# Four cross-attention layers: the wide layers' values multiplied with the output weights before the probabilities are

## The chip, the cores and the metric

The kernel runs on one core of one Trainium2 chip. The metric is the device time of one execution in microseconds. Three runs of the kernel before took 2065.84 to 2066.42 us, with a median of 2066.3 us.

## What is computed

The stream `x` has 8 batches of 512 tokens with 512 channels, the context 8 batches of 77 rows with 1024 channels. Four layers follow each other. Layers 0 and 2 are the wide ones (16 heads of 64, a token bias, an output bias), 1 and 3 the narrow ones (16 heads of 32, four groups of keys and values, a root-mean-square norm on the queries' side).

```
def wide(x, ctx):                      # L0, L2
    q, k, v = heads64(x @ Wq), heads64(ctx @ Wk), heads64(ctx @ Wv)
    probs = softmax(q @ k.T * 64 ** -0.5 + col_bias)
    return merge(probs @ v) @ Wo + bo + x
def narrow(x, ctx):                    # L1, L3
    q, k, v = heads32(rmsnorm(x) @ wq), groups4(ctx @ wk), groups4(ctx @ wv)
    return merge(softmax(q @ k.T * 32 ** -0.5) @ v) @ wo + x
```

All is float32 in the reference. The kernel splits each operand into a high part in fp32r and a rest, and multiplies in three passes: high by high, high by rest, rest by high.

## The kernel before

**Context phase.** `context_part` runs nine rounds `j`: eight form the keys and values of four heads of a wide layer (`k_scr`, `v_scr` in DRAM), the ninth those of both narrow layers. In a round TensorE makes four key chains (banks 0 to 3, 8 channel chunks of 3 passes of 308 columns each: 96 multiplications) and five value chains (banks 4 to 7, 8 chunks of 3 passes of 256 columns: 120 multiplications). ScalarE copies a bank's high part out (`drain_keys`, `drain_values`) and VectorE forms the rest; both also split the next round's weights, which SyncE loads. In round 0 VectorE forms the token bias (a chain of 39 small instructions on lines 498 to 516) before it drains the first keys. Only the start of round 1 waits for these key drains.

**Main phase.** 128 units `u`, 32 to a layer: a batch has four units of four heads. Step `s` of the program holds the scores of unit `s` (four tiles of 128 tokens by 4 x 77 columns), the queries of unit `s+1`, the transposes of unit `s-1`, and probabilities times values of unit `s-2`. Each engine has its order written out by hand. For a unit TensorE makes

- scores: 24 multiplications of 154 columns (wide) or 12 of 308 (narrow),
- queries: 24 or 12 of 512 columns,
- transposes (`turn`): three blocks of four, 128 columns each; the third block holds the columns that don't fit into the first two,
- probabilities times values (`values`): 8 of 512 columns in either kind,
- the output projection (`project`): 96 in a wide batch, 48 in a narrow one, of 512 columns.

VectorE subtracts the maxima (`tile_scores`), forms the denominators, and the rests of queries, transposes and head outputs (`rest_q`, `rest_t`, `rest_o`), and adds the result to the stream (`add_result`). ScalarE makes the exponentials and the high parts. GpSimd normalises the probabilities (`normalise`), gathers the third block of wide units (`rest`) and forms the rests of the stream and of weights. A transpose waits for the bank's readers two transposes before; a score tile waits for VectorE's subtraction two tiles before, and in wide layers also for ScalarE's bias (`s_biased`). The exponentials of a narrow layer wait for `rstd`, which GpSimd makes after TensorE's `stats`. In narrow steps the addition of a projection is left to the next step (`late`).

## Time and profile before

| | |
|---|---|
| median of three runs | 2066.3 us |
| the profiled execution, its own time | 2066.7 us |
| its span, first to last instruction | 2064.9 us |
| mean granted clock of TensorE | 0.996 |
| context phase | 0 to 262 us |
| layers 0, 1, 2, 3 begin (first scores) | 268, 782, 1148, 1681 us |
| TensorE busy | 2024.2 us, 98% |
| VectorE, ScalarE, GpSimd busy | 68%, 47%, 31% |

Matmuls are pipelined, and the busy time of one is longer than its distance to the next; the distances between starts are what adds up. PE is TensorE's multiplications, PEld its weight loads, DVE VectorE, ACT ScalarE, POOL GpSimd, SPq the DMA issues of SyncE.

### The profile page before, as it was taken

To read this page: it belongs to the slowest core of one execution; us is meant where nothing else is said; L and a number is where in the kernel's file an instruction comes from. 1 tells how busy PE (TensorE), PEld (TensorE's weight loads), DVE (VectorE), ACT (ScalarE), POOL (GpSimd) and SP (SyncE) were. 2 spreads that over 40 slices of the span, in tenths; PEclk is the share of its full clock that TensorE was granted. 3 is DMA by queue.
4 is the path that set the end of the run, shared out by engine and by line. 5 is a ranking of instruction groups with operands and counts; after the bars stand their busy time and mean duration, and the time that the engine had idled before them with its cause. 6 is when DMAs were issued, how large, how long until landed. Compare 5 with 4: busy or idle time off the path is not lost.

```text
span 2064.9 us, 31181 instructions
## 1 busy us (share of the span) xinstructions
PE 2024.2 (98%) x11482; PEld 1760.5 (85%) x11482; DVE 1398.2 (68%) x2408; ACT 966.0 (47%) x1814; POOL 649.5 (31%) x534
## 2 busy tenths in 40 slices
PE   8999999999999998999999999999999989999998
PEld 8999988888888887788888888888888877888887
DVE  5332365775577557788888676557755775888886
ACT  3222354544355354555555454345443553555553
POOL 1000043311232244454444431223122543444441
PEclk9999999999999999999999999999999999999999
DMA  7889742222122222343333332222221222333332
GB/s 196 183 176 200 191 97 67 68 65 79 51 72 71 70 71 74 89 107 100 87 98 94 101 96 68 72 60 67 66 79 52 72 77 81 74 92 92 88 72 84
DMA packets 262537, 191.02 MB, mean 93 GB/s; under 512 B 197522, under 2 KB 199986, under 8 KB 259826
## 3 DMA queue, kind: packets, MB, share of 16 engines
q1 hardware_dynamic: 262386, 189.03, 35.7%
q8 instruction: 92, 1.51, 0.3%
q14 instruction: 59, 0.48, 0.1%
HBM read 132.66 MB, written 56.26 MB: 91 GB/s over the span
## 4 chain that ended last, share of the span: by engine, by line
PE 48%; issue 30%; POOL 11%; DVE 6%; ACT 2%; DMA 1%; SPq 1%; POOLq 0%; DVEq 0%; ACTq 0%
PE acc_bank L877 6%; POOL prob L1311 6%; PE acc_bank L261 4%; PE t_bank L857 4%; PE acc_bank L263 4%; PE acc_bank L262 4%; PE q_bank L835 4%; PE q_bank L837 3%; PE q_bank L839 3%; PE ctx_bank L261 3%; PE ctx_bank L262 3%; PE ctx_bank L263 3%; POOL x_s L1286 3%; PE s_bank L261 2%; POOL rest L1320 2%
## 5 line engine op out<-in xcount | busy, mean ns | idle before, releaser
L1311 POOL TENSOR_TENSOR prob<-prob,rinv 128x1232 f32<-128x1232 f32 x128 | 288.3, 2252 | 1006.3 <-DVE rinv L1195 1006.2
L1053 ACT ACTIVATE q_s<-q_bank 128x512 fp32r<-128x512 f32 x192 | 114.7, 597 | 489.3 <-PE q_bank L839 486.2
L877 PE MATMUL acc_bank<-pT_s,vals_s 128*128 128x512 f32 x1024 | 337.8, 415 | 0.0
L835 PE MATMUL q_bank<-x_s,w_s 128*128 128x512 f32 x768 | 319.4, 416 | 0.0
L1153 DVE TENSOR_REDUCE mx<-s_bank 128x4 f32<-128x308 f32 x512 | 240.1, 469 | 108.6 <-PE s_bank L801 54.3
L837 PE MATMUL q_bank<-x_s,w_s 128*128 128x512 f32 x768 | 313.3, 408 | 0.0
L839 PE MATMUL q_bank<-x_s,w_s 128*128 128x512 f32 x768 | 313.1, 408 | 0.0
L261 PE MATMUL acc_bank<-o_s,w_s 128*128 128x512 f32 x752 | 300.4, 400 | 2.8 <-DVE o_s L1186 2.5
L263 PE MATMUL acc_bank<-o_s,w_s 128*128 128x512 f32 x752 | 293.6, 390 | 0.0
L262 PE MATMUL acc_bank<-o_s,w_s 128*128 128x512 f32 x752 | 293.1, 390 | 0.0
L1044 ACT ACTIVATE prob<-prob,rstd 128x308 f32<-128x308 f32 x256 | 140.7, 553 | 263.2 <-DVE prob L1157 238.0
L1157 DVE TENSOR_TENSOR prob<-s_bank,mx 128x308 f32<-128x308 f32 x512 | 245.0, 478 | 27.4 <-DVE mx L1153 1.4
L1180 DVE TENSOR_TENSOR pT_s<-t_bank,pT_s 128x512 fp32r<-128x512 f32 x256 | 175.6, 686 | 78.5 <-ACT pT_s L1067 78.5
L877 PEld LDWEIGHTS acc_bank<-pT_s,vals_s 128*128 128x128 f32 x1024 | 191.0, 189 | 28.1
L1209 DVE SCALAR_TENSOR_TENSOR x_back<-acc_bank,bo,x_back 128x512 f32<-128x512 f32 x64 | 47.8, 748 | 244.9 <-PE acc_bank L263 244.9
L1067 ACT ACTIVATE pT_s<-t_bank 128x512 fp32r<-128x512 f32 (+1 forms) x320 | 183.1, 589 | 34.3 <-PE t_bank L857 34.2
L857 PE MATMUL t_bank<-ident,prob 128*128 128x128 f32 (+1 forms) x1280 | 184.7, 273 | 1.2 <-DVE pT_s L1180 1.2
L1192 DVE TENSOR_REDUCE sums<-prob 128x16 f32<-128x1232 f32 x128 | 182.5, 1426 | 0.0
L857 PEld LDWEIGHTS t_bank<-ident,prob 128*128 128x128 f32 (+1 forms) x1280 | 154.6, 135 | 28.0 <-DVE pT_s L1180 1.6
L261 PEld LDWEIGHTS acc_bank<-o_s,w_s 128*128 128x128 f32 x752 | 141.4, 188 | 31.2 <-DVE o_s L1186 4.4
L263 PEld LDWEIGHTS acc_bank<-o_s,w_s 128*128 128x128 f32 x752 | 141.2, 188 | 30.6
L839 PEld LDWEIGHTS q_bank<-x_s,w_s 128*128 128x128 f32 x768 | 145.5, 189 | 23.0
(107 smaller groups left out, 4092.8 us busy)
## 6 DMA issues: line engine op xcount, KB each, us to landing
stream<-x_back SPq DMA_DIRECT2D x128, 256.0 KB, 2.6
x_front<-stream SPq DMA_DIRECT2D x96, 256.0 KB, 3.3
x_back<-stream SPq DMA_DIRECT2D x96, 256.0 KB, 4.0
kvw_raw<-kvw SPq DMA_DIRECT2D x17, 1024.0 KB, 8.4
k_scr<-k_out SPq DMA_DIRECT2D x36, 308.0 KB, 10.5
keys_s<-k_scr SPq DMA_DIRECT2D x128, 77.0 KB, 2.5
v_scr<-v_out SPq DMA_DIRECT2D x8, 1024.0 KB
vals_s<-v_scr SPq DMA_DIRECT2D x512, 6.5 KB
```

The lines of the kernel that those rows point to most:

```text
L261: pe.matmul(out, weights[0], moving[0], start=start, stop=False)
L262: pe.matmul(out, weights[0], moving[1], start=False, stop=False)
L263: return pe.matmul(out, weights[1], moving[0], start=False, stop=stop)
L835: pe.matmul(out, w[0], x_now[0], start=k == 0, stop=False)
L837: pe.matmul(out, w[0], x_now[1], start=False, stop=False)
L839: mm = pe.matmul(out, w[1], x_now[0], start=False, stop=k == XC - 1)
L857: mm = pe.transpose(t_bank[(3 * u + n) % 2][0:rows, t * P:t * P + P], p, ident[:, :])
L877: mm = pe.matmul(out, w, pT_s[:, part], start=i == mine[0] and part == 2 * n and w is v[0], stop=i == mine[-1] and w is terms[-1][0] and p ...
L1067: act.activation(pT_s[0:rows, 2 * n], t_bank[(3 * u + n) % 2][0:rows, :], ACT.Copy).then_inc(t_hi, 1)
L1153: dve.tensor_reduce(top, scored, AX_X, ALU.max).then_inc(s_max, 1)
L1157: dve.tensor_tensor(prob[:, slot, t].rearrange("q (h n) -> q h n", h=GH), scored, top.unsqueeze(2).broadcast_to([P, GH, CTX]), ALU.subtrac ...
L1311: pool.tensor_tensor(view, view, rinv[:, slot].unsqueeze(2).broadcast_to([P, TILES * GH, CTX]), ALU.mult).then_inc(p_norm, 1)
```

## The change

In the wide layers (probs @ v) @ Wo becomes probs @ (v @ Wo), head by head. The product v @ Wo has 4 x 77 rows of 512 columns for each batch and group of four heads. It is formed for all batches in the context phase and kept in DRAM.

- **Context, rounds 0 to 7.** The five value chains go. Four chains like the keys' give the values turned, in the key chains' banks 0 to 3: chain n waits until the drain of key chain n of the same round is done (`k_lo`), and the next round's key chain n for the turned values' drain (`vt_lo`). The high part of a head lies in 64 partitions and its rest in the other 64, with Wo in both, so that two multiplications give all four products.
- **Context, rounds 1 to 8.** Between the chain steps TensorE makes 20 outputs of the round before (5 row blocks, 4 heads), two multiplications of 512 columns each, in banks 4 to 7. ScalarE drains the even ones, VectorE the odd ones into a ring of three 1 MB blocks, from which SyncE stores them. That is 616 x 4 rows of 2048 bytes for a round, 5.05 MB. Wo is loaded and split once for a round. The keys are stored with 2464 bytes in a row (308 before). Round 8 keeps five value chains for the narrow layers, in banks 0 to 3. The ring lies where the first query weights go afterwards, so that their split waits for its last stores.
- **Wide layers.** `project` and `values` go. Two units are taken together: their 616 probability rows make five blocks (four of 128, one of 104), and for each of four output chunks TensorE makes 15 multiplications of 512 columns, 60 for two units. Half of a pair's chunks stand in each of steps u+3 and u+4. SyncE loads 256 columns of the product for both units, ScalarE and GpSimd split two chunks of 640 columns for a step (`split_rows`, `rest_rows`), VectorE adds the bank to the stream (`add_wide`). `rest_o` and `split_o` go there. The value products now stand beside the scores of tiles 0 and 1, the queries beside those of tiles 2 and 3. Steps 0 to 2 and 64 to 66 have none.
- **Transposes, all layers.** The third block of two units is transposed together, after the second: 20 transposes for two units (24 before). GpSimd gathers it for narrow units too. In a narrow pair VectorE takes two pieces of 64 partitions out of the shared bank; the even unit's last two value products wait for it, and its drain moves to the next step.
- **Narrow additions.** `late` holds for odd steps only; in even steps VectorE adds the projection at the step's end.
- **Weights.** Wo of the wide layers is no longer streamed in the main phase.

```diff
 
-WEIGHTS = [("woA0", 0, 2, (0, 0, 1, 1)), ("woA1", 0, 3, (2, 2, 3, 3)),
-           ("wqB", 0, 0, (29, 29, 29, 29)), ("woB", 0, 1, (32, 33, 34, 35)),
-           ("wqA0", 1, 2, (36, 37, 38, 39)), ("wqA1", 1, 3, (40, 41, 42, 43)),
-           ("woA0", 1, 0, (63, 64, 65, 65)), ("woA1", 1, 1, (67, 67, 68, 68)),
-           ("wqB", 1, 2, (93, 93, 93, 93)), ("woB", 1, 3, (96, 97, 98, 99))]
+WEIGHTS = [("wqB", 0, 2, (12, 13, 14, 15)), ("woB", 0, 3, (16, 17, 18, 19)),
+           ("wqA0", 1, 0, (37, 38, 39, 40)), ("wqA1", 1, 1, (41, 42, 43, 44)),
...
+    def wide(self, s):
+
+        u = (s - 3) // 2 * 2
+        if not 0 <= u < NU or kind(u).name == "B":
+            return []
+        return [(u, 2 * (s - 3 - u) + i) for i in range(2)]
...
+    def split_values(self, u):
+
+        return self.narrow(u) and u % 2 == 0
+
+    def turns(self, u):
+
+        if not 0 <= u < NU:
+            return ()
+        if u % 2 == 0:
+            return 0, 1
+        return (0, 1, TWICE) if kind(u).name == "A" else (0, TWICE, 1)
...
+    def outs_after(j, step):
+
+        if j == 0:
+            return []
+        return [i for i in range(OUTS) if (8 + 5 * i // 2 if j < LAST else 6 + 3 * i // 2) == step]
+
...
+        def store_rows(j, r):
+            block = NV * j + r
+            sp.wait_ge(vw_act, 2 * block + 2)
+            sp.wait_ge(vw_dve, 2 * block + 2)
+            for b, t0, t1, row in ROW_PIECES[r]:
+                sp.dma_start(vw_scr[j, b, :, t0:t1].rearrange("h t c -> t h c"),
+                             staged[row:row + t1 - t0, block % 3].rearrange("p (h c) -> p h c", h=GH))\
+                  .then_inc(vw_stored[block % 3], 16)
+
...
+
+            act.wait_ge(wo_loaded, 32 * (j + 1))
+            if j:
+                act.wait_ge(vw_mm, OUTS * j)
+            act.activation(wd[:, 0], wo_raw[:, :], ACT.Copy).then_inc(wo_hi, 1)
 
         def drain_keys(n, j):
...
+        def drain_turned(n, j):
+
+            m, into, cols = n // 2, vt[j % 2], slice(n % 2 * HALF, (n % 2 + 1) * HALF)
+            act.wait_ge(vt_mm, 4 * j + n + 1)
+            if n == 0 and j >= 2:
+                act.wait_ge(vw_mm, OUTS * (j - 1))
+            act.activation(into[0:64, 2 * m, cols], banks[n][0:64, 0:HALF], ACT.Copy)
+            act.activation(into[64:P, 2 * m + 1, cols], banks[n][64:P, 0:HALF], ACT.Copy).then_inc(vt_hi, 1)
+
+        def drain_outputs(j, outs):
+
+            for i in outs:
+                if i % 2 == 0:
+                    block, h = NV * (j - 1) + i // GH, i % GH
+                    act.wait_ge(vw_mm, OUTS * (j - 1) + i + 1)
+                    if h == 0 and block >= 3:
+                        act.wait_ge(vw_stored[block % 3], rows_stored(block - 3))
+                    rows = VROWS[i // GH]
+                    act.activation(staged[0:rows, block % 3, 512 * h:512 * h + 512], banks[4 + i % 4][0:rows, :], ACT.Copy)\
+                       .then_inc(vw_act, 1)
...
+                act.wait_ge(vw_mm, OUTS * (LAST - 1))
+            elif n == 1:
+                act.wait_ge(wo_lo, LAST)
+                for block in range(NV * LAST - 3, NV * LAST):
+                    act.wait_ge(vw_stored[block % 3], rows_stored(block))
             act.activation(late_parts(n)[0], w_raw[:, n % 2], ACT.Copy).then_inc(late_hi, 1)
...
+        def chain_step(slot, n, k):
+
...
+        def outputs(j, step):
+
+            for i in outs_after(j, step):
+                r, h = divmod(i, GH)
+                if i == 0:
+                    pe.wait_ge(vt_lo, 4 * j)
+                    pe.wait_ge(wo_lo, j)
+                before = OUTS * (j - 1) + i - 4
+                if before >= 0:
+                    pe.wait_ge(vw_dve if i % 2 else vw_act, before // 2 + 1)
+                out = banks[4 + i % 4][0:VROWS[r], :]
+                v = vt[(j - 1) % 2][:, h, r * P:r * P + VROWS[r]]
+                pe.matmul(out, v, wd[:, 0, 512 * h:512 * h + 512], start=True, stop=False)
+                pe.matmul(out, v, wd[:, 1, 512 * h:512 * h + 512], start=False, stop=True).then_inc(vw_mm, 1)
...
+                chain_step(0, n, k)
         for j in range(NJ):
+            step = 0
             if j:
                 pe.wait_ge(w_lo[0], j)
-                pe.wait_ge(k_lo, 4 * j)
                 for n in range(4):
+                    pe.wait_ge(vt_lo, 4 * (j - 1) + n + 1)
                     for k in range(KC):
-                        keys(n, k)
+                        chain_step(0, n, k)
+                        outputs(j, step)
+                        step += 1
+            else:
+                step = 4 * KC
             pe.wait_ge(w_lo[1], j + 1)
-            for r in range(NV):
-                values(r, j)
+            if j < LAST:
+                for n in range(4):
+                    pe.wait_ge(k_lo, 4 * j + n + 1)
+                    for k in range(KC):
+                        chain_step(1, n, k)
+                        outputs(j, step)
+                        step += 1
+            else:
+                for r in range(NV):
+                    if r < 4:
+                        pe.wait_ge(k_lo, 4 * j + r + 1)
+                    else:
...
+                    sp.wait_ge(acc_mm, plan.acc[("pv", u - 2, 0)] + 1)
                 vals = vals_s[:, slot].bitcast(F32)
-                for h, t0, t1, blk, row, (first, last) in kind(u).pieces:
...
+            def load_rows(s):
+
+                if not plan.wide(s):
+                    return
+                u, m = plan.wide(s)[0]
+                half, b, p = plan.chunk(u, m) // 2, u // GROUPS % B, u // (2 * UNITS)
+                if half >= 2:
+                    sp.wait_ge(rows_lo, 2 * half - 2)
+                if u % UNITS == 0:
+                    sp.wait_ge(rows_zeroed, u // (2 * UNITS) + 1)
+                into, cols = rows_s[:, half % 2], slice(P * m, P * (m + 2))
+                for e in range(2):
+                    src = vw_scr[4 * p + (u + e) % GROUPS, b].rearrange("h t c -> (h t) c")
+                    sp.dma_start(into[:, 2 * e:2 * e + 2], src[0:2 * P, cols].rearrange("(n q) c -> q n c", q=P))\
+                      .then_inc(rows_loaded[half % 2], 16)
+                    sp.dma_start(into[REST * e:REST * (e + 1), 4], src[2 * P:SC, cols])\
+                      .then_inc(rows_loaded[half % 2], 16)
 
...
-                    pe.wait_ge(p_gathered, plan.gathered(u))
+                    if u == 0:
+                        pe.wait_ge(context.v_lo, len(VROWS))
+                item = plan.t[(u, n)]
+                after(pe, t_lo, item - 1)
+                if n == TWICE:
+                    pe.wait_ge(p_gathered, u + 1)
...
+            def wide_values(s):
+
+                for u, m in plan.wide(s):
+                    n, item = plan.chunk(u, m), plan.acc[("pv", u, m)]
...
-                            mm = pe.matmul(out, w, pT_s[:, part], start=i == mine[0] and part == 2 * n and w is v[0],
-                                           stop=i == mine[-1] and w is terms[-1][0] and part == terms[-1][1])
-                            if i == mine[-1] and w is terms[-1][0] and part == terms[-1][1]:
-                                mm.then_inc(acc_mm, 1)
...
+                        if m == 0:
+                            pe.wait_ge(t_lo, wide_turn(u, block) + 1)
+                        rows, p = BROWS[block], wide_block(u, block)
+                        w = [ring(n)[0:rows, h, block] for h in range(2)]
+                        pe.matmul(out, w[0], p[0:rows, 0], start=block == 0, stop=False)
+                        yield
+                        pe.matmul(out, w[0], p[0:rows, 1], start=False, stop=False)
+                        yield
+                        mm = pe.matmul(out, w[1], p[0:rows, 0], start=False, stop=block == BLOCKS - 1)
+                        if block == BLOCKS - 1:
...
                     for t in range(TILES):
                         beside(scores(s, t), q, 6)
-                        if t >= 2:
-                            turned(t - 2)
-                    turned(2)
+                        if t == 2:
+                            turned(turns[:2])
+                    turned(turns[2:])
                 elif a:
                     half = 12 if kind(s + 1).name == "A" else 6
-                    beside(scores(s, 0), q, half)
-                    beside(scores(s, 1), q, half)
-                    beside(scores(s, 2), v, 4)
-                    turned(0)
-                    beside(scores(s, 3), v, 4)
-                    turned(1)
-                    turned(2)
-                    for gb, m in plan.projections(s):
-                        project(gb, m)
+                    run(wide, 6)
+                    run(v, 6 if behind else 8)
+                    beside(scores(s, 0), wide, 12)
+                    beside(scores(s, 1), wide, 12)
+                    beside(scores(s, 2), q, half)
+                    if not behind:
+                        projected(projections)
+                    turned(turns[:2])
+                    beside(scores(s, 3), q, half)
+                    turned(turns[2:])
                     if plan.stats_at(s) is not None:
                         stats(plan.stats_at(s))
+                    if behind:
+                        projected(projections[:1])
+                        run(v, 2)
...
-                    turned(1)
+                    run(v, 3 if behind else 5)
+                    turned(turns[1:2])
                     if plan.stats_at(s) is not None:
                         stats(plan.stats_at(s))
-                    turned(2)
-                    if not plan.ahead(s):
-                        for gb, m in plan.projections(s):
-                            project(gb, m)
+                    turned(turns[2:])
+                    if behind:
+                        projected(projections[:1])
+                        run(v, 2)
+                        projected(projections[1:])
+                    else:
+                        projected(projections)
                 elif s == NU:
-                    run(v, 9)
-                    for gb, m in plan.projections(s):
-                        project(gb, m)
-                    turned(0)
...
+            def split_rows(n):
+
+                act.wait_ge(rows_loaded[n // 2 % 2], 64 * (n // 4 + 1))
+                if n >= CHUNKS:
+                    act.wait_ge(acc_mm, plan.chunk_item(n - CHUNKS) + 1)
+                if n // (2 * UNITS) and n % (2 * UNITS) < CHUNKS:
+                    act.wait_ge(acc_mm, plan.acc[("proj", 2 * B - 2, XC - 1)] + 1)
+                act.activation(ring(n)[:, 0], raw_rows(n), ACT.Copy).then_inc(rows_hi, 1)
 
...
+            def add_wide(u, m):
+
+                item, gb, p = plan.acc[("pv", u, m)], u // GROUPS, u // (2 * UNITS)
                 out, here = acc_bank[item % 2][:, :], x_back[:, m]
-                if kind(GROUPS * gb).name == "A":
+                dve.wait_ge(acc_mm, item + 1)
+                if u % GROUPS == 0:
+                    dve.wait_ge(back_loaded[m], 16 * (gb + 1))
                     dve.scalar_tensor_tensor(out=here, in0=out, scalar=bo[:, p, m:m + 1], in1=here,
                                              op0=ALU.add, op1=ALU.add).then_inc(acc_out, 1)
                 else:
+                    dve.wait_ge(acc_out, plan.acc[("pv", u - 2, m)] + 1)
                     dve.tensor_tensor(here, out, here, ALU.add).then_inc(acc_out, 1)
 
...
+                        rest_o(s - 2)
+                    tile_scores(s, 2)
+                    if kind(s + 1).name == "A":
                         next(q, None)
-                    tile_scores(s, 1)
+                    if not behind:
+                        added(projections)
+                    turned(turns[:2])
+                    tile_scores(s, 3)
                     next(q, None)
-                    tile_scores(s, 2)
-                    if pv == 2:
-                        rest_o(s - 2, 0)
-                    turned(0)
-                    tile_scores(s, 3)
-                    turned(1)
-                    if pv:
-                        rest_o(s - 2, pv - 1)
...
-                    if s >= 1 and not plan.rest_later(s - 1):
-                        rest_t(s - 1, TWICE)
...
+                        add_wide(u, m)
+                    turned(turns[:1])
+                    if s < NU and not wide:
                         denominators(s)
                     next(q, None)
                     next(q, None)
...
+                    turned(turns[2:])
+                    added(projections)
             for m in range(XC):
                 dve.wait_ge(end_mm, m + 1)
...
+                if u >= 2:
+                    pool.wait_ge(t_mm, plan.rest_read_before(u))
+                size = REST if kind(u).name == "A" else REST_B
+                pool.tensor_copy(rest[:, :, size * slot:size * slot + size], prob[:, slot, :, SC - size:SC])\
+                    .then_inc(p_gathered, 1)
+
+            def rest_rows(n):
+
+                pool.wait_ge(rows_hi, n + 1)
+                pool.tensor_tensor(ring(n)[:, 1], raw_rows(n), ring(n)[:, 0].bitcast(F32), ALU.subtract).then_inc(rows_lo, 1)
 
```

## Rows read from the trace of the kernel before

**Rows 1.** The page's first part: busy time, share of the span, instructions of each engine.

```profile
PE 2024.2 (98%) x11482; PEld 1760.5 (85%) x11482; DVE 1398.2 (68%) x2408; ACT 966.0 (47%) x1814; POOL 649.5 (31%) x534
```

**Rows 2.** Busy time by stretch: stretch, length, each engine (instructions), granted clock, DMA share, GB/s.

```profile
80.00:160.00 80.00, 80.00 (x626) 80.00 (x626) 24.85 (x32) 21.28 (x32) 0.00 (x0) 1.00 0.85 175
867.00:1076.00 209.00, 208.66 (x1123) 178.12 (x1122) 178.56 (x322) 119.34 (x223) 103.55 (x72) 1.00 0.37 98
...
407.00:474.35 67.35, 67.35 (x369) 57.85 (x368) 44.84 (x77) 30.64 (x60) 17.00 (x17) 1.00 0.25 68
```

**Rows 3.** Timeline of TensorE, context phase: start, us, engine, line, tiles, count.

```profile
23.45 0.28 PE L261 MATMUL ctx_bank<-w_s,ctx_s 128*128 128x256 f32 x1
...
66.92 0.30 PE L261 MATMUL ctx_bank<-ctx_s,w_s 128*128 128x308 f32 x1
...
80.53 0.28 PE L261 MATMUL ctx_bank<-w_s,ctx_s 128*128 128x256 f32 x1
...
94.71 0.31 PE L261 MATMUL ctx_bank<-ctx_s,w_s 128*128 128x308 f32 x1
```

**Rows 4.** Timeline of TensorE, main phase: 24 query multiplications, eight transposes, what follows.

```profile
262.16 0.40 PE L835 MATMUL q_bank<-x_s,w_s 128*128 128x512 f32 x1
...
267.64 0.23 PE L795 MATMUL s_bank<-keys_s,q_s 128*128 128x154 f32 x1
...
1158.52 1.04 PE L857 MATMUL t_bank<-ident,prob 128*128 128x128 f32 x8
1159.31 0.48 PE L261 MATMUL acc_bank<-o_s,w_s 128*128 128x512 f32 x1
```

**Rows 5.** Timeline of ScalarE, then of VectorE, in the first context round.

```profile
22.39 1.70 ACT L415 ACTIVATE k_out<-ctx_bank 128x308 fp32r<-128x308 f32 x4 [4.61 <-PE ctx_bank L263]
23.98 1.91 ACT L408 ACTIVATE w_s<-kvw_raw 128x2048 fp32r<-128x2048 f32 x1
...
31.66 0.30 DVE L516 SCALAR_TENSOR_TENSOR bias_s<-ctx_raw,mask_b,bias_s 128x77 f32<-128x77 f32 x1
32.00 1.64 DVE L464 TENSOR_TENSOR k_out<-ctx_bank,k_out 128x308 fp32r<-128x308 f32 x4
33.55 2.28 DVE L458 TENSOR_TENSOR w_s<-kvw_raw,w_s 128x2048 fp32r<-128x2048 f32 x1
```

**Rows 6.** Groups by shape, 0 to 400 us: count | busy, mean ns | idle before.

```profile
L261 PE MATMUL ctx_bank<-ctx_s,w_s 128*128 128x308 f32 x288 | 89.0, 309 | 7.5 <-DVE ctx_s L484 7.5
...
L261 PE MATMUL ctx_bank<-w_s,ctx_s 128*104 128x256 f32 x72 | 20.3, 282 | 1.4 <-DVE v_out L470 1.2
```

**Rows 7.** Busy time by stretch, around the first narrow unit of layer 1.

```profile
784.50:788.10 3.60, 0.10 (x2) 0.03 (x1) 3.39 (x8) 0.00 (x0) 2.98 (x3) 0.90 0.19 38
788.10:794.60 6.50, 6.50 (x20) 5.45 (x21) 4.29 (x8) 2.58 (x5) 1.23 (x2) 0.53 0.13 28
```

**Rows 8.** DMA busy tenths and GB/s in 40 slices of 0 to 280 us; issues: us to landing.

```profile
DMA  6954199995998199949992999299959953949931
GB/s 212 417 186 150 39 113 188 368 108 93 338 201 62 78 337 256 98 105 353 177 69 96 358 161 75 113 342 345 106 145 344 150 44 136 334 117 174 142 95 51
...
kvw_raw<-x_in SPq DMA_DIRECT2D x1, 1024.0 KB, 6.9
```

**Rows 9.** Timeline of VectorE, one narrow unit of layer 3 (idle before, and its releaser).

```profile
2011.43 0.48 DVE L1153 TENSOR_REDUCE mx<-s_bank 128x4 f32<-128x308 f32 x1 [0.49 <-PE s_bank L263]
...
2016.68 0.69 DVE L1180 TENSOR_TENSOR pT_s<-t_bank,pT_s 128x512 fp32r<-128x512 f32 x1 [0.51 <-ACT pT_s L1067]
2017.29 1.43 DVE L1192 TENSOR_REDUCE sums<-prob 128x16 f32<-128x1232 f32 x1
...
2020.77 0.69 DVE L1177 TENSOR_TENSOR pT_s<-t_bank,pT_s 64x512 fp32r<-64x512 f32 x1
...
2021.89 0.48 DVE L1153 TENSOR_REDUCE mx<-s_bank 128x4 f32<-128x308 f32 x1 [0.44 <-PE s_bank L263]
```

**Rows 10.** Timeline of TensorE: the second unit of layer 0 begins.

```profile
279.21 0.34 PE L795 MATMUL s_bank<-keys_s,q_s 128*128 128x154 f32 x1 [1.49 <-DVE q_s L1164]
```

791 lines of the change are left out of this document (447 added, 344 removed).

## The prediction

> **What bounds the kernel now.** I read the page's first part, then the busy time by stretch, then TensorE's timeline for the distances between starts, and last what TensorE waits for. TensorE is busy in 98% of the span [rows 1]. In the context phase it has no gap, nor in a steady wide batch (67.35 us), and in the narrow stretch 0.3 us of 209 [rows 2]. So the first thing to count is TensorE's instructions, at their distance from start to start; the second is who makes it wait in the 40.7 us of its idle time (2064.9 less 2024.2 [rows 1]), 7.5 of which are the first loads [rows 6].
>
> The distances: 96 key multiplications of 308 columns take 80.53 - 66.92 = 13.61 us, 0.142 each; 120 of 256 columns 94.71 - 80.53 = 14.18 us, 0.118 each [rows 3]. 24 of 512 columns take 267.64 - 262.16 = 5.48 us, 0.228 each; eight transposes and what follows them 0.79 us, so 0.109 for each distance between transposes and 0.03 from the last to another kind [rows 4].
>
> **TensorE's count, context.** Removed: 8 rounds x 120 x 0.118 = 113.3 us. Added: 8 x 96 x 0.142 = 109.1, and 8 rounds x 20 outputs x 2 x 0.228 = 73.0. Together +68.8 us. Nothing hides it: this stretch has no gap to fill [rows 2].
>
> **TensorE's count, main phase.** A wide unit loses 8 value and 24 projection products and gets 30, so 2 x 0.228 = 0.456 us less, over 64 units 29.2. All 128 units lose two transposes on average, 256 x 0.109 = 27.9 us. Together -57.1 us. The count alone therefore gives +68.8 - 57.1 = +11.7 us. The product saves little because its inner length is 308 per four heads where the head outputs' is 256; it pays off by what other engines lose, and those don't set the time now.
>
> In two sentences apart: the Trainium skill ("TensorE: Matmul & The Clock Gate", section "Back-to-back issue gap") gives columns / 2.4 + 2.5 ns, which is 216, 131, 109 and 56 ns for 512, 308, 256 and 128 columns where the trace has 228, 142, 118 and 109. By these the count would be +64.8 - 42.0 = +22.8 us; its section "LDWEIGHTS" (128 columns in 107 ns) agrees with the 109 of the transposes.
>
> **A new wait in round 0.** The turned values' chain n uses the bank of key chain n and waits for VectorE's drain of it. ScalarE has its part done at 24.0, but VectorE comes to its first key drain only at 32.00, behind the token bias [rows 5]. Before, the value chains had banks of their own and started at 23.45 [rows 3]. Now TensorE stands from 23.45 to 32.00 + 0.48 + about 0.1: 9.1 us. Queued behind are all its later work, and so everybody. After 3.6 us without work TensorE ran at half clock (1.2 GHz) for most of the next 6.5 us, granted 0.53 [rows 7]; that costs 6.5 x 0.47 = 3.1 us here too. The 1.4 us that the fifth value chain waited for a bank [rows 6] goes. Sum +10.8. Bounds: 0, if I misread the order, and +12.2, if the 1.4 stays.
>
> **Other waits in the context phase.** Each output has a wait on its bank's drain four outputs earlier, about 6 us; the longest that stands before it on either engine is a weight split, 1.91 + 2.28 [rows 5], so it is hidden in rounds 1 to 7. In round 8 the first stream tile is split ahead of the output drains. Its load is issued after the stores of round 7's last block and takes 6.9 us [rows 8]; TensorE has 3.4 us of steps left in the round (8 of 0.42) and then some 7 to its fifth output, while load and both halves of the split take 1.8 + 6.9 + 1.91 + 2.28 = 12.9. Drain and order on two engines make it +3.5, bounds 0 and +6. The stores: a round moves 5.05 MB of products, 2 of weights, 1 of Wo and 1.26 of keys, 9.3 MB in 36.5 us, 255 GB/s. Slices of this phase reached 338 to 417 [rows 8], so I take 0, and 3 us a round (+24) as the upper bound. SyncE waits for a block's drains with a weight load queued behind it; that load has 20 us of slack.
>
> **Wide layers, steady.** VectorE loses two head rests and a transpose rest per unit, ScalarE likewise; GpSimd gets about 3.3 us for two chunks, at 52 us busy in a wide batch's 67 before only 17.0 [rows 2]. The copies of a chunk are made a step ahead. A first product block waits for the third transpose's rest, which I place 1.3 us before it is needed. 0, bounds 0 and +9.
>
> **Narrow layers, steady.** A pair of units has 2 x 10.46 = 20.9 us (2021.89 - 2011.43 for one [rows 9]) and TensorE's share falls by 4 x 0.109 = 0.44. VectorE has 0.44 to 0.49 us to spare where a unit begins [rows 9]. In the even step it now takes two pieces of 64 partitions (0.69 each) instead of one, has the addition at the end instead of in the next step, and has lost one head rest: 0.7 us more in front of the next unit's maxima. That is 0.3 over its slack and meets a TensorE that is earlier by 0.1. I take 0.35 us of waiting in a pair, 28 pairs: +10. Bounds 0 and +20. So the narrow transposes' gain (half of 27.9) comes back for the most part.
>
> **Borders of the layers.** (a) Wide to narrow, twice: TensorE now waits 3.5 us at the first narrow unit and then runs at half clock [rows 7]. After the change the 1.4 us of rest copies and two more rests are gone from VectorE's tail, and 6.8 us of value products stand in each of the first three narrow steps. The wait falls to about 2, perhaps short enough to keep the clock: -7 each, -14. Bounds -20 and 0. (b) Narrow to wide, once: steps 64 to 66 have score tiles 0 and 1 with nothing beside them, and tile 2 waits for maxima, subtraction and bias of tile 0: 1.2 us in two of them, 3.5 in the one without narrow value products, less what is lost there now: +5, bounds +2 and +9. (c) Step 2 loses its value products. A unit there waited 1.49 us for its queries' rest [rows 10]: +1.6, bounds 0 and +3.
>
> **The sum**, against the profiled execution's 2066.7 us (span and 1.8 around it, 0.4 over the median): +11.7 + 10.8 + 3.5 + 0 + 10 - 14 + 5 + 1.6 = +28.6. It gives 2095.3, and as a median 2095 us, 1.4% slower.
>
> **The rivals.**
> - *The setup wait is hidden.* If VectorE reaches the key drains before TensorE needs them, 10.8 falls away: 2084. Against it stands VectorE's unbroken timeline up to 32.00 [rows 5]. Chance 0.12.
> - *The stores come late.* 5 MB a round in a ring of three blocks; where a store lands over 12 us after its drain, ScalarE and VectorE stop, and TensorE with them. At 2.5 us a round, +20: 2115. For it speaks that slices are full already [rows 8], against it that the key stores become eight times as long a run. Chance 0.12.
> - *VectorE sets the narrow layers.* It was busy 178.6 of 209 us [rows 2], and even steps get more. With 1.0 us of waiting for a pair instead of 0.35, +18 to +20: 2114. Chance 0.13.
> - *A transpose is not worth its distance.* If removing one gives back only the 0.03 us between kinds, the saving is 7 us instead of 27.9: 2116. The rows say otherwise, as transposes follow each other at 0.109 throughout. The Trainium skill's figure of the second part would put this rival at 2106. Chance 0.03.
> - *Faster: the other engines' relief empties the main phase of waits.* One mechanism, at the layers' borders: VectorE and ScalarE lose some 2 us in each wide unit, and if TensorE then nowhere waits, up to 40.7 - 7.5 - 1.4 = 31.8 us of idle time and 2 x 3.1 of half clock go. With the count (+11.7) and round 0 (+10.8) that gives 2051 at the utmost. It decides from 26.6 us of released waiting on (the 22.5 and the bound of 4.1); for that the borders' new holes and the narrow pairs must cost nothing. I set it at 2057. Chance 0.06, and 0.04 for stopping on the way, at 2066.
> - *The forecast:* 0.50.
>
> **Range and chances.** Two kernels can be told apart by about 0.2%, 4 us. The forecast's own low end takes the lower bounds of several terms, about 2074; its high end with the ring or the narrow layers at their bounds about 2122. The range 2074 to 2122 leaves out the faster case and the tails. Faster 0.06, within 0.2% 0.04, slower 0.90.
>
> **What would show it.** The first scores should move from 267.6 [rows 4] to 267.6 + 68.8 + 10.8 + 3.5 = 351 us. TensorE should have 2.7 us less in a steady wide batch, 64.6 instead of 67.35. A gap of 9 us must stand at 23.5 with VectorE's key rest as its releaser and half clock behind it. In narrow layers the gaps should come in every second unit, at tile 3, released by VectorE. If the stores were late, ScalarE's waits in rounds 1 to 8 would name the stores. The prediction is wrong if the context phase is not longer by 70 us or more, or if a wide batch doesn't get shorter.

## The result, and the profile after

The kernel after takes 2362.5 us (median of four runs, 2359.4 to 2368.1), the kernel before in the same job 2066.4. The ratio is 1.1435, with a 95% interval of 1.1411 to 1.1459. I had forecast 2095 us, 2074 to 2122. The direction was right; of 296 us more, 29 were foreseen.

The page of after, in its parts: busy time of the first part (answers [rows 1]); TensorE's busy tenths, its granted clock and the DMA share of the second part in 40 slices; three groups of the fifth.

```profile
PE 2122.7 (90%) x11226; PEld 1814.4 (77%) x11226; DVE 1387.9 (59%) x2360; ACT 1000.1 (42%) x1814; POOL 823.1 (35%) x643
...
PE   7979876799978899989898999988999998898988
...
PEclk9989987899989899999999999998999999999999
DMA  5766765322232233323323233322333333233222
...
L1082 PE MATMUL acc_bank<-pT_s,vals_s 128*128 128x512 f32 x512 | 152.4, 411 | 65.7 <-issue 56.4
...
L259 PE MATMUL ctx_bank<-ctx_s,w_s 128*128 128x308 f32 x544 | 170.7, 314 | 17.3 <-DVE k_out L552 10.3
...
L1319 ACT ACTIVATE o_s<-rows_s 128x640 fp32r<-128x640 f32 x128 | 93.2, 730 | 207.2 <-DMA rows_s<-vw_scr 204.6
```

TensorE is busy in 90% of a longer span: 243 us idle where it had 41. The holes are in three places of the tenths: the first eight slices (context phase), slices 12 to 14 (part of layer 0) and 27 and 28 (part of layer 2), and a little everywhere in the narrow layers. The span is 2366.1 us, 301.2 over before's 2064.9. By the first score of each layer, the parts are:

| | before | after | difference | forecast |
|---|---|---|---|---|
| first scores | 267.6 | 446.6 | +179.0 | +83.1 |
| wide layers 0, 2 | 514.5, 532.5 | 550.7, 563.4 | +67.2 | -36.6 |
| narrow layers 1, 3, with the end | 365.9, 384.4 | 394.3, 411.0 | +55.0 | -18.0 |

(Forecast, wide: -29.2, half of the transposes -14.0, +5, +1.6. Narrow: -14.0, +10, -14.) So all three parts went wrong, and each needs its own cause.

**Context phase.** First the stretch of 50 to 440 us by busy time (columns as in [rows 2]), then what waited in the first 450 us (engine, line, what for: us in total, times, longest), then two rows of TensorE's timeline: the gap of round 0, and the first scores.

```profile
50.00:440.00 390.00, 310.87 (x1876) 290.40 (x1875) 153.77 (x200) 130.03 (x200) 0.00 (x0) 0.89 0.63 199
```

```profile
ACT staged L488 <- DMA vw_scr<-staged: 139.9, 24, 18.4
...
PE ctx_bank L689 <- ACT staged L488: 67.3, 8, 14.1
PE s_bank L1162 <- DVE wq_s L583: 11.4, 1, 11.4
```

```profile
32.62 0.60 PE L259 MATMUL ctx_bank<-ctx_s,w_s 128*128 128x308 f32 x1 [10.30 <-DVE k_out L552]
...
446.59 0.23 PE L1003 MATMUL s_bank<-keys_s,q_s 128*128 128x154 f32 x1
```

TensorE, which had no gap in the 80 us of this phase that [rows 2] shows, is idle for 79 of 390 us. In 67.3 of them, eight waits of up to 14 us, it waits for ScalarE's drain of an output; ScalarE waits for the ring's stores. The other 11.4 us stand at the end of the phase: the split of the first query weights, which go where the ring was, waits 12.2 us on ScalarE for the ring's last stores. The DMA engines' mean share is 0.63 (the row's last number but one): by that number they are far from full, and the stores are late all the same. That contradiction is what the experiments had to settle. The gap of round 0 is there as forecast, 10.3 us for 9.1, behind VectorE's key rest; from 32.6 to 37.4 us the granted clock is 0.50.

**Layers 0 and 2.** A steady wide batch takes 559.08 - 493.95 = 65.13 us from start to start (67.35 before, 64.6 forecast), so the change does what it was to do there. But units 13 to 20 of layer 0, in which weights are split, take 18 to 25 us in place of 16. One of them, in the order of the cause: GpSimd's weight rest, SyncE's issues, ScalarE's copy of a product chunk, TensorE's next score tile.

```profile
671.32 1.32 POOL L1577 TENSOR_TENSOR w_s<-stage,w_s 128x512 fp32r<-128x512 f32 x1
```

```profile
672.66 0.34 SPq L929 DMA_DIRECT2D stage<-wqB  x1
...
673.99 0.46 SPq L918 DMA_DIRECT2D rows_s<-vw_scr  x1
```

```profile
680.04 0.74 ACT L1319 ACTIVATE o_s<-rows_s 128x640 fp32r<-128x640 f32 x1 [11.37 <-DMA rows_s<-vw_scr]
```

```profile
681.15 0.49 PE L1003 MATMUL s_bank<-keys_s,q_s 128*128 128x154 f32 x1 [5.80 <-ACT s_bank L1264]
```

SyncE issues the next weight piece when GpSimd's rest of the piece two before is done (672.64), and only behind it the loads of the product's rows. They land at 680.0. ScalarE has stood for them for 11.4 us, and the bias of a score tile, which TensorE needs, is queued behind that copy: 5.8 us.

**Narrow layers.** A pair of units takes 24.6 us (1100.60 to 1125.18; the steady ones 23.0 to 25.0) where before it took 20.9 to 21.7. The even unit begins at 1100.60, the odd one at 1115.01 (TensorE), and between them stand this gap of TensorE and this addition of VectorE:

```profile
1100.60 0.30 PE L259 MATMUL s_bank<-keys_s,q_s 128*128 128x308 f32 x1
...
1106.02 1.62 PE L1082 MATMUL acc_bank<-pT_s,vals_s 128*128 128x512 f32 x3 [2.08 <-issue]
...
1115.01 0.30 PE L259 MATMUL s_bank<-keys_s,q_s 128*128 128x308 f32 x1
```

```profile
1104.85 0.48 DVE L1410 TENSOR_TENSOR prob<-s_bank,mx 128x308 f32<-128x308 f32 x1
1105.24 0.68 DVE L1462 TENSOR_TENSOR x_back<-acc_bank,x_back 128x512 f32<-128x512 f32 x1
```

The profile names no releaser ("issue"), but the product starts 0.1 us after VectorE's addition of the step before ends (1105.92). In an even unit the last accumulator item ahead of the value products is the projection of the step before, whose addition is `late`: VectorE makes it behind all four score tiles. The gap is not at tile 3, where I had looked for it, but behind it.

### The profile page after: what moved, and what is told of

It reads as the page before. It is cut to its first block, busy times and chain, and to the rows that moved or that the text cites. A ratio compares the mean times of both kernels' runs of the same rounds, so it can differ in the third digit from the quotient of the medians.

```text
span 2366.1 us, 30805 instructions
## 1 busy us (share of the span) xinstructions
PE 2122.7 (90%) x11226; PEld 1814.4 (77%) x11226; DVE 1387.9 (59%) x2360; ACT 1000.1 (42%) x1814; POOL 823.1 (35%) x643
## 4 chain that ended last, share of the span: by engine, by line
PE 65%; DMA 11%; issue 8%; POOL 5%; SPq 5%; DVE 3%; ACT 2%; DVEq 0%; POOLq 0%; ACTq 0%
PE q_bank L1045 6%; PE q_bank L1047 6%; PE q_bank L1049 6%; DMA vw_scr<-staged 6%; PE acc_bank L1082 5%; PE t_bank L1066 5%; PE acc_bank L1099 5%; PE acc_bank L1103 5%; PE acc_bank L1101 5%; DMA rows_s<-vw_scr 3%; PE acc_bank L259 2%; PE acc_bank L261 2%; PE acc_bank L260 2%; SPq L381 2%; PE s_bank L259 2%
## 5 line engine op out<-in xcount | busy, mean ns | idle before, releaser
L1596 POOL TENSOR_TENSOR o_s<-rows_s,o_s 128x640 fp32r<-128x640 f32 x128 | 198.1, 1566 | 173.7 <-ACT o_s L1319 173.6
L1045 PE MATMUL q_bank<-x_s,wq_s 128*128 128x512 f32 x512 | 222.9, 435 | 0.0
L1047 PE MATMUL q_bank<-x_s,wq_s 128*128 128x512 f32 x512 | 221.8, 433 | 0.0
L1049 PE MATMUL q_bank<-x_s,wq_s 128*128 128x512 f32 x512 | 221.1, 432 | 0.0
L1264 ACT ACTIVATE s_bank<-bias_s 128x308 f32<-128x308 f32 x256 | 111.5, 436 | 259.0 <-DVE prob L1410 258.1
L1082 PE MATMUL acc_bank<-pT_s,vals_s 128*128 128x512 f32 x512 | 152.4, 411 | 65.7 <-issue 56.4
L1417 DVE TENSOR_TENSOR q_s<-q_bank,q_s 128x512 fp32r<-128x512 f32 x192 | 129.1, 673 | 110.9 <-ACT q_s L1288 97.4
L1003 PE MATMUL s_bank<-keys_s,q_s 128*128 128x154 f32 x512 | 129.5, 253 | 64.4 <-ACT s_bank L1264 62.2
L259 PE MATMUL ctx_bank<-ctx_s,w_s 128*128 128x308 f32 x544 | 170.7, 314 | 17.3 <-DVE k_out L552 10.3
L1319 ACT ACTIVATE o_s<-rows_s 128x640 fp32r<-128x640 f32 x128 | 93.2, 730 | 207.2 <-DMA rows_s<-vw_scr 204.6
L260 PE MATMUL ctx_bank<-ctx_s,w_s 128*128 128x308 f32 x544 | 170.2, 313 | 0.0
L261 PE MATMUL ctx_bank<-ctx_s,w_s 128*128 128x308 f32 x544 | 169.7, 312 | 0.0
L1003 PEld LDWEIGHTS s_bank<-keys_s,q_s 128*128 128x128 f32 x512 | 98.9, 193 | 88.7 <-ACT s_bank L1264 67.0
L1559 POOL TENSOR_TENSOR x_s<-x_front,x_s 128x512 fp32r<-128x512 f32 x124 | 158.9, 1303 | 2.3 <-ACT x_s L1245 2.3
L1099 PE MATMUL acc_bank<-o_s 128*128 128x512 f32 x384 | 158.2, 412 | 0.0
```

The source lines that it names most:

```text
L259: pe.matmul(out, weights[0], moving[0], start=start, stop=False)
L260: pe.matmul(out, weights[0], moving[1], start=False, stop=False)
L261: return pe.matmul(out, weights[1], moving[0], start=False, stop=stop)
L1003: pe.matmul(cols, q_s[:, slot, 0, c, tok], keys[:, c, 0], start=False, stop=False, skip_group_check=True)
L1045: pe.matmul(out, w[0], x_now[0], start=k == 0, stop=False)
L1047: pe.matmul(out, w[0], x_now[1], start=False, stop=False)
```

## The experiments

Each experiment changes the kernel after in one place (unless it says otherwise) and was timed beside the kernel before on the same chip.

**1. Blocks stored whole.** One transfer for a block of 128 or 104 rows instead of two or three cut at batches. The rows land in another order, so the wide layers multiply with rows in the wrong place; the amount of work is the same.

```diff
-            for b, t0, t1, row in ROW_PIECES[r]:
-                sp.dma_start(vw_scr[j, b, :, t0:t1].rearrange("h t c -> t h c"),
-                             staged[row:row + t1 - t0, block % 3].rearrange("p (h c) -> p h c", h=GH))\
-                  .then_inc(vw_stored[block % 3], 16)
+            flat = vw_scr[j].rearrange("b h t c -> (b h t c)").rearrange("(r n) -> r n", n=GH * D)
+            sp.dma_start(flat[r * P:r * P + VROWS[r]], staged[0:VROWS[r], block % 3])\
+              .then_inc(vw_stored[block % 3], 16)
```

> The changed kernel, but each block of V times Wo (128 rows, or 104, of 8192 bytes) is stored by one transfer instead of two or three pieces of 77, 51, 26, 25, 76, ... rows. The bytes and their run lengths stay near (same 5.05 MB a round); the rows land in another order, so the wide layers multiply with rows in the wrong place. Theory (pieces with an odd number of rows are served by few DMA engines): TensorE's 67.3 us of waits for ScalarE's drains and the 11.4 us at the context phase's end go, with most of the half clock behind them; the first scores start at 350 to 375 us instead of 446.6, the time is 2270 to 2300 us. Rival (the 40 MB of writes to DRAM are simply too much at this rate): as many bytes, so first scores stay at 430 or later and the time above 2345.

Measured: 2272.9 us, ratio 1.0996 (1.0964 to 1.1027). The stretch of 50 to 350 us, the two waits that answer to those of after, and the first scores:

```profile
50.00:350.00 300.00, 296.51 (x1887) 280.52 (x1886) 154.97 (x201) 131.54 (x201) 0.53 (x1) 0.99 0.75 259
```

```profile
PE ctx_bank L259 <- DVE k_out L551: 9.5, 1, 9.5
ACT staged L487 <- DMA vw_scr<-staged: 4.1, 1, 4.1
```

```profile
351.73 0.23 PE L1002 MATMUL s_bank<-keys_s,q_s 128*128 128x154 f32 x1
```

The waits for stores fall from 139.9 to 4.1 us, the wait of 11.4 us for the query weights is gone, and the first scores come at 351.7, where the prediction's sum has 351. So the whole error of the context phase, 95 us, is in how the stores are cut. This edit changes two things, though: over how many DMA engines a store goes, and that a row is written as 8 KB in one run instead of four of 2 KB.

**2. Pieces cut at multiples of 16 rows.** The first of the two things alone.

```diff
-            pieces.append((b, lo - b * CTX, hi - b * CTX, lo - r * P))
+            cut = lo + (hi - lo) // 16 * 16
+            for a, z in ((lo, cut), (cut, hi)):
+                if a < z:
+                    pieces.append((b, a - b * CTX, z - b * CTX, a - r * P))
```

> The kernel after, and each piece of a stored block cut once more, at the last multiple of 16 rows: 23 transfers a round instead of 12, the same rows to the same places, still 2 KB at a time. The experiment that stored whole blocks changed two things, over how many DMA engines a store is split and how long its contiguous runs in DRAM are (8 KB for 2 KB); this one changes the first alone. Theory, too few engines for a store: a piece of 77 rows goes over 11 engines, one of 51 over 3, one of 1 over 1, and the lowest-numbered engine has 688 KB of a round's stores where an even share is 315 KB; cut like this it has 360 KB. The stores then land in the round: the wait of ScalarE's drains for the stores (139.9 us) falls below 30 us, TensorE's wait for these drains (67 us) below 10 us, the first scores come at 350 to 365 us and the time is 2270 to 2295 us. Rival, the pieces are too many and too small (2 KB runs, one more transfer each on SyncE's queue): with 23 for 12 nothing gets better, the first scores stay at 440 us or come later, and the time is 2355 us or more.

Measured: 2285.8 us, ratio 1.106 (1.1026 to 1.1095). ScalarE's wait for the stores, the stretch, the first scores:

```profile
ACT staged L491 <- DMA vw_scr<-staged: 21.4, 7, 6.7
```

```profile
50.00:350.00 300.00, 293.76 (x1863) 277.61 (x1863) 150.33 (x197) 126.90 (x195) 0.00 (x0) 0.99 0.88 259
```

```profile
361.90 0.23 PE L1006 MATMUL s_bank<-keys_s,q_s 128*128 128x154 f32 x1
```

With nearly twice as many transfers (23 for 12), 85 of the 95 us are back. The rival, that the pieces are too many and too small, is out; what the edit changed is the row counts, and so, by the theory, the number of engines. A smaller part is left: the same 259 GB/s take 0.88 of the engines' time with 2 KB runs and 23 stores a round, and 0.75 with 8 KB runs and 5. The last 10 us go with the run length or with the number of transfers; these two were not told apart.

**3. The rule by itself.** Experiment 1, and the first block of a round in two transfers, 127 rows and 1.

```diff
+    def cuts(r):
+        return ((0, 127), (127, 128)) if r == 0 else ((0, VROWS[r]),)
...
-            sp.dma_start(flat[r * P:r * P + VROWS[r]], staged[0:VROWS[r], block % 3])\
-              .then_inc(vw_stored[block % 3], 16)
+            for a, z in cuts(r):
+                sp.dma_start(flat[r * P + a:r * P + z], staged[a:z, block % 3]).then_inc(vw_stored[block % 3], 16)
```

> The experiment with blocks stored whole (first scores 351.7 us, 2273 us; its wide layers multiply with rows in the wrong place, and so do this one's), and of the five blocks of a round the first is stored in two transfers, of 127 rows and of 1. The bytes, the rows and the 8 KB runs are the same, and there is one more transfer a round (6 for 5). Theory, the number of engines is the largest divisor of the row count up to 16: 127 rows go to one engine. That engine then has 1.04 MB of this block, 0.24 MB of the other four and 0.28 MB of the loads and key stores in a round, 1.56 MB. In the kernel after, the busiest engine had 0.97 MB a round, and a round took 36.5 + (446.6 - 351.7) / 8 = 48.4 us, 20 GB/s; by this rate a round here takes 78 us, the first scores come 330 us later, at about 680 us (620 to 760), and the time is about 2600 us. Rival, the length of the runs and the number of transfers are what matters: nothing changes beyond 2 us a round, the first scores come before 370 us and the time is 2290 us at most.

Measured, one run: 2530.6 us. The DMA share in tenths and the GB/s in 40 slices of 50 to 600 us, one of these slices by itself (its last two numbers: DMA share, GB/s), TensorE's wait, and the first scores:

```profile
DMA  6132580505913258050670506914148041550505
GB/s 169 57 141 97 166 263 28 211 27 188 258 63 158 81 179 250 27 201 37 196 232 27 212 27 210 297 71 167 72 158 267 30 175 63 170 210 27 208 28 194
```

```profile
132.50:146.25 13.75, 12.03 (x76) 11.10 (x74) 4.06 (x4) 3.31 (x4) 0.00 (x0) 1.00 0.07 28
```

```profile
PE ctx_bank L691 <- ACT staged L490: 239.9, 9, 33.0
```

```profile
610.42 0.23 PE L1005 MATMUL s_bank<-keys_s,q_s 128*128 128x154 f32 x1
```

One transfer more in a round costs 259 us. Slice after slice shows 27 or 28 GB/s at a share of 0 tenths; by itself such a slice has a share of 0.07, and one engine of 16 is 0.06. So a single engine is at work, and this is its rate. The theory holds for 127 rows; the size was off (610 us, under my 620 to 760), because I had taken 20 GB/s for an engine from the kernel after. At 27, the 1.04 MB of the odd transfer take 38.5 us, more than a round's 36.5 by itself. With its part of the other four blocks (0.26 MB, not the 0.24 of the expectation) and 0.28 MB of loads and keys this engine has 1.58 MB, an estimate of 59 us for a round; 36.5 + 258.7 / 8 = 69 us were measured. Some 10 us a round stay open.

With that the kernel after can be read. Its pieces of a round have 77, 51; 26, 77, 25; 52, 76; 1, 77, 50; 27, 77 rows, and by the largest divisor up to 16 they go to 11, 3; 13, 11, 5; 13, 4; 1, 11, 10; 9, 11 engines. If one engine is in all of them, it has 688 KB of the 5.05 MB, 0.28 MB of other transfers beside it, and an even share would be 315 KB. This is an estimate by the rule, since the profile doesn't name the engine of a transfer. At the 27 GB/s of this experiment its 0.97 MB are 36 us, as much as a round of 36.5 has; the kernel after took 48.4 for a round on the average, which is 20 GB/s. So the count says that this engine is full, but not why a round takes 12 us more than at 27 GB/s. An engine's rate with rows of 2 KB was not measured alone.

The Trainium skill states this rule ("DMA: Bandwidth & Descriptors", section "Why a DMA increments its semaphore by 16 and not by 1"): a transfer runs on the largest k up to 16 that divides the slowest dimensions of both sides, the lowest-numbered k engines, so 127 partitions go to one. The runs here agree with it on the number of engines for 127 rows (a share of 0.07 at 28 GB/s), and by experiment 2 for the kernel after as a whole; which engines a transfer takes, no run here shows. I had not weighed it.

**4. The product's rows ahead of the weight pieces,** on SyncE's queue.

```diff
+                load_rows(s + 2)
                 if s < NU and kind(s).name == "A":
                     for n in plan.pieces(s):
                         if n + 2 < len(PIECES):
                             load_weights(n + 2)
...
-                load_rows(s + 2)
```

> The changed kernel, but SyncE issues the rows of step s+2 before the weight pieces of step s. Theory (SyncE stands at a weight load until GpSimd has made the rest of the piece two before, which comes late in a step, and the rows behind it come late): the slow wide steps, eight of 18 to 25 us in layer 0 and six in layer 2, become 16.1 to 16.5; 47.7 + 37 = 85 us less, 2275 to 2290. Rival (in these steps ScalarE or GpSimd has too much work with the pieces themselves): the steps stay above 18 us and the time above 2330.

Measured: 2263.0 us, ratio 1.0948 (1.088 to 1.1015). ScalarE's group of chunk copies, of the fifth part's kind:

```profile
L1319 ACT ACTIVATE o_s<-rows_s 128x640 fp32r<-128x640 f32 x128 | 93.0, 728 | 56.0 <-DMA rows_s<-vw_scr 53.4 <-PE acc_bank L1103 2.5
```

ScalarE's waits for rows fall from 204.6 to 53.4 us. All units of layer 0 from the fourth to the last but one take 16.06 to 16.51 us, and the wide layers 502.1 and 524.4 us instead of 550.7 and 563.4: -88. The rest of the 99.5 us, and of the time being under my 2275, is mostly in a context phase that was 10.7 us shorter in this run (first scores 435.9). That phase scatters from run to run while the stores are late: the first scores come at 443.5 in the next experiment, which doesn't touch it.

**5. The late addition ahead of the score tiles,** on VectorE, in narrow steps.

```diff
                 else:
+                    for gb, m in plan.late(s - 1):
+                        add_result(gb, m)
                     if s < NU:
                         for t in range(TILES):
                             tile_scores(s, t)
-                    for gb, m in plan.late(s - 1):
-                        add_result(gb, m)
```

> The changed kernel, but in narrow steps VectorE adds the projection that the step before left to it ahead of the four score tiles, not behind them. Theory (the even step's value products take the bank of that projection's accumulator only after the addition, 2.2 us too late, 26 times, with half clock behind some): narrow pairs fall from 23 to 24.6 us to 20.5 to 21.5, 45 to 60 us less, 2300 to 2320. Rival (VectorE's load sets the narrow pair whatever its order): pairs stay at 22.5 or more and the time above 2345.

Measured: 2290.6 us, ratio 1.1081 (1.1049 to 1.1113). The first score tile of an odd unit, of the even one behind it and of the next odd one, then the group of value products:

```profile
1059.52 0.30 PE L259 MATMUL s_bank<-keys_s,q_s 128*128 128x308 f32 x1
...
1069.70 0.30 PE L259 MATMUL s_bank<-keys_s,q_s 128*128 128x308 f32 x1
...
1080.45 0.30 PE L259 MATMUL s_bank<-keys_s,q_s 128*128 128x308 f32 x1
```

```profile
L1082 PE MATMUL acc_bank<-pT_s,vals_s 128*128 128x512 f32 x512 | 145.3, 396 | 11.8 <-DVE pT_s L1431 9.4 <-issue 2.4
```

The two units take 20.93 us (the next two 21.3), and TensorE's idle time ahead of these products falls from 65.7 to 11.8 us. The narrow layers lose 74.7 us (45 to 60 expected), 54 of them waiting; the other 21 go with the half clock behind some of the gaps (the even unit had 12.9 or 14.4 us, now 10.75; behind the gap shown above, from 1106 to 1110 us, the granted clock was 0.58). So it was not that VectorE was too busy, which was my rival for these layers, but where one instruction stood.

**6. The token bias behind the key drains of round 0,** on VectorE: the 39 small instructions move behind that round's first weight split.

```diff
         for j in range(LAST):
             for n in range(4):
                 drain_outputs(j, outs_in_chain(j, n))
                 drain_keys(n, j)
             split_weights(0, j + 1)
+            if j == 0:
+                token_bias()
...
```

> The changed kernel, but VectorE forms the token bias after the key drains and the first weight split of round 0, not before them. Theory (the 10.5 us gap at 22 us is the wait for the first key rest): the gap goes, a shorter one of 2 to 5 us may stand at the start of round 1; the first scores come 5 to 14 us earlier if the stores leave that to be seen, time 2348 to 2360. Rival (the stores set the context phase, so what is gained in round 0 is waited for later): gap gone, first scores within 3 us of 446.6, time unchanged.

Measured: 2346.9 us, ratio 1.1354 (1.127 to 1.1437; the two runs are 14 us apart). The one gap of TensorE that is left in 20 to 60 us:

```profile
40.69 0.60 PE L259 MATMUL ctx_bank<-ctx_s,w_s 128*128 128x308 f32 x1 [3.89 <-DVE x_s L561]
```

The wait of 10.3 us turns into one of 3.9, now for the rest of the turned values, which is behind the bias instead. What it is worth can't be read here, since the stores' waits scatter by more: in this profiled execution the first scores came at 415.1, 31.5 us earlier than in the kernel after, with a wait that is 6.4 us shorter. In experiment 7 it can.

**7. The four edits together,** with blocks stored whole, and then with pieces at multiples of 16 rows (which computes all that the reference does).

> Four edits at once: blocks stored whole (rows of the product in another order, so that the wide layers multiply with rows in the wrong place), the product's rows loaded ahead of the weight pieces, the projection of a narrow step added ahead of its score tiles, and the token bias formed behind the key drains of round 0. Theory, the four causes are separate places of the path and their gains add up: by the single runs 90 + 100 + 72 + 16 = 278 us, so 2363 - 278 = 2085 us, first scores at 345 us, a wide layer 500 us less 28 where its narrow border is, a narrow one 356 and 371 us. Rival, the causes share their stalls (SyncE's queue serves the stores, the rows and the weights): the gains overlap by 50 us or more and the time is 2135 us or more. By the forecast's own sum without the round-0 wait it would be 2084 us; if it comes out above 2100 us, another term of the forecast was wrong too.

> The same four edits, with the pieces cut at multiples of 16 rows in place of whole blocks: it computes all that the reference does. Theory: within 10 us of the one with whole blocks, 2080 to 2100 us, which is slower than before by 0.7 to 1.6%, because the context phase takes 80 us more (first scores at 345 to 355 us, 268 us before), and the main phase gives back 60 us. Rival: the change can be had at a gain once its waits are gone: below 2062 us.

Measured: 2111.4 us, ratio 1.0216 (1.0196 to 1.0237), and 2115.2 us, ratio 1.0242 (1.0225 to 1.0259). The stretch of 50 to 350 us and the first scores of the second one:

```profile
50.00:350.00 300.00, 292.17 (x1842) 275.80 (x1841) 150.34 (x195) 128.48 (x196) 0.53 (x1) 0.98 0.87 258
```

```profile
352.63 0.23 PE L1010 MATMUL s_bank<-keys_s,q_s 128*128 128x154 f32 x1
```

251 and 247 of the 296 us are gone, so the four causes are most of the miss. My 278 was too much: it had added single medians, in which the scatter of the context phase was counted twice. By the parts, 95 (context) + 88 (rows) + 75 (narrow) + 5 (bias, 351.7 to 346.9 with whole blocks) = 263. From span to span, as these parts are read, 256 us are gone in the first kernel, 69 of them in the narrow layers. So the gains add up within 7 us, and the rival, an overlap of 50 us or more, is out. Both kernels are slower than expected (2085, and 2100 at most): another term of the forecast was wrong too. The second one lies 20 us over my 2095 and is slower than before by 49 us. Its rival, a gain once the waits are gone, is out.

**8. What the borders are worth without the change.** With the waits out, the two narrow layers are 10.1 and 8.4 us shorter than before's, most of it at the wide-to-narrow borders, where before TensorE waits 3.5 us and runs at half clock [rows 7]. Is that the change, or only an order? Here the kernel *before* is edited: in the first two narrow steps behind a wide layer, TensorE takes all queries ahead of tile 2, and VectorE the mean squares and a block's rest behind tile 1.

```diff
-                    run(q, half)
+                    run(q, 2 * half if plan.border(s) else half)
...
                         for t in range(TILES):
                             tile_scores(s, t)
+                            if t == 1 and plan.border(s):
+                                if s % UNITS == 0:
+                                    mean_squares(plan.stats_at(s - 1))
+                                rest_t(s - 2, TWICE)
...
```

> The kernel before, unchanged in context phase and layers but for the first two narrow steps behind a wide layer: TensorE takes all 12 query multiplications ahead of score tile 2 (6 before), and VectorE takes score tiles 0 and 1 ahead of the mean squares and of the 1.39 us of rest copies. It asks whether what the kernel after gains at the borders (its narrow layers are 10 and 8 us shorter than before's once its waits are out) needs the change at all. Theory, it is the order there: before has a wait of 3.50 us at the first narrow unit with half clock behind it (3.1 us), and one of 1.65 at the second. VectorE's first tile comes 2.1 us earlier and 1.37 us of queries fill the rest, so both waits go, twice: 2 x (3.5 + 3.1 + 1.7) = 16 us at most; since the half clock may stay where a shorter wait does, I expect 6 to 14 us, 2053 to 2061 us, faster than before by 0.3 to 0.7%. Rival, the waits move: the value products then wait for the rest copies by as much, and the time is within 0.2% of before, 2063 to 2070 us.

Measured: 2069.0 us, ratio 1.0017 (1.0008 to 1.0026). TensorE's timeline at the border, and ScalarE's:

```profile
787.22 0.41 PE L265 MATMUL s_bank<-keys_s,q_s 128*128 128x308 f32 x1 [0.21 <-DVE prob L1161]
...
793.20 1.12 PE L861 MATMUL t_bank<-ident,rest 128*128 128x128 f32 x4 [2.11 <-DVE pT_s L1184]
```

```profile
789.92 1.88 ACT L1048 ACTIVATE prob<-prob,rstd 128x308 f32<-128x308 f32 x4 [5.55 <-POOL rstd L1337]
791.83 0.60 ACT L1071 ACTIVATE pT_s<-t_bank 128x512 fp32r<-128x512 f32 x1
```

The wait of 3.5 us is down to 0.2 and has come up again at the third block's transposes, 2.1 us, with half clock behind it. The releaser named is VectorE, but VectorE waits for ScalarE's copy at 791.83, and that stands behind the exponentials, which wait for GpSimd's `rstd`. From 793.2 to 796 us the granted clock is 0.50. The rival came true in the time and in that the wait moved, though to the transposes and not to the value products.

**9. The same, with ScalarE's copies ahead of its exponentials** (the queries and the first transposed block, in the first narrow step; in that step VectorE also takes the queries' rest ahead of the block's, and TensorE takes all queries ahead of tile 2 in that step alone).

```diff
+                    if plan.first(s) and s < NU:
+                        next(q, None)
+                        turned(0)
                     if s < NU:
                         exps(s, 0)
                         exps(s, 1)
...
-                    turned(0)
+                    if not plan.first(s) or s >= NU:
+                        turned(0)
...
```

> The kernel before with its first two narrow steps reordered further. The first border experiment took TensorE's waits of 3.50 and 1.65 us away and got one of 2.11 at the third block's transposes (793.20), 1.10 behind it and longer ones in the second step instead: these transposes wait for VectorE's rest of the first block, which waits for ScalarE's copy of it, and that copy stands behind the four exponentials, which wait for GpSimd's rstd until 789.9 us. Here ScalarE copies the queries and the first transposed block ahead of the exponentials in the first narrow step, VectorE takes the queries' rest ahead of the block's, and TensorE takes all queries ahead of tile 2 in that step alone. Theory, the order on ScalarE was the last thing that held these steps: the copy can start at 789.1, the transposes come 1.5 to 3 us earlier, twice, and in the second step 1.4 us of the 1.65 stay gone: 2056 to 2063 us, faster by 0.15 to 0.5%. Rival, the path runs over rstd and the exponentials themselves (square sums, transposes, mean squares, power, 1.9 us of exponentials, denominators, normalise), which no order of the copies shortens: 2065 to 2070 us.

Measured: 2063.4 us (eleven runs, 2060.9 to 2064.8), before 2066.0, ratio 0.9984 (0.9975 to 0.9993).

```profile
791.98 0.65 PE L865 MATMUL t_bank<-ident,rest 128*128 128x128 f32 x4 [1.26 <-DVE pT_s L1192]
...
796.67 0.41 PE L269 MATMUL s_bank<-keys_s,q_s 128*128 128x308 f32 x1 [1.79 <-DVE prob L1169]
```

The first unit of each narrow layer takes 10.2 us instead of 14.3 and 14.0, and the second one gives most of it back (24.2 and 25.5 for 22.6). 2.6 us are left, 0.13%, between my two ranges: the only version here that is below before, by less than the 4 us that I would call different. Why the second unit is longer was not followed further. In the kernel with the waits out (experiment 7, the second one) the first six units of the narrow layers are 10.5 and 8.5 us shorter than before's. The two orders tried in the kernel before gave nothing and 2.6 us in all, so most of that gain was not to be had by these orders; another order is not excluded.

## Why the prediction was wrong

**The stores: the term that failed first.** The prediction put them at 0, bounds 0 and +24, by holding 255 GB/s against slices of 338 to 417 [rows 8]. Measured: +95. The step is wrong in kind. A mean over 16 engines doesn't tell whether one of them is full; the number to ask for was the share of the fullest engine, by the rule 688 KB of stores in a round and not 315. That the cut of the stores cost these 95 us is shown (experiment 1), that a transfer of 127 rows has one engine too (experiment 3); how 688 KB make just 95 us stays open. The rows for it were in the diff (pieces of 51, 76 and 1 rows), not in the trace: before stored its values by 128 rows. The rival "the stores come late" had the right place, but 2.5 us a round where 11.9 were lost, so its 2115 was nearly as far off as the rest.

**"That load has 20 us of slack."** I followed SyncE's queue for one load and one phase. In the main phase the same queue has a new customer, the product's rows, behind weight pieces that wait for a GpSimd rest, and GpSimd now makes it behind the normalise. Measured: +88 in the two wide layers. The term "wide layers, steady: 0 to +9" held for steady batches (65.13 us), but steps with weights were not among them.

**Narrow layers, steady: +10, bounds 0 and +20.** The engine was right (VectorE, even steps), and the mechanism was wrong: I added up its work and looked at tile 3. What counted was the order of the accumulator's items: the value products' item stands behind the projection's, whose addition was left to the next step behind four tiles. Measured: 54 us of waiting and 21 of half clock. With all four edits (the second kernel of experiment 7) the two narrow layers together are 18.5 us shorter than before, and my sum for them was 18.0. That is in part luck: of the 14 us for transposes only 2.8 show in the 24 steady units of each layer, though TensorE waits for nothing there (209.69 of 210 us busy); the first six units of each give 19.0 and the last two take 3.3 back.

**What held.** The count of the context phase: 83.1 forecast, 84.1 with blocks stored whole. The gap of round 0 (9.1 plus half clock; 10.3 and half clock). The +3.5 of round 8 (2.2 and 1.3 us of waits for output drains with blocks stored whole). By the formula that the Trainium skill gives for a single multiplication apart from others ("TensorE: Matmul & The Clock Gate", section "Back-to-back issue gap") the context phase would have been longer by 79.1, an estimate; for a sustained stream the same section has about 131 ns at 512 columns, where the trace has 228. So here the rows were the better price. The rival on transposes needs more care than I gave it: with it a wide batch would be 65.3 us, where my count had 64.65, and 65.13 were measured. From the starts of one batch (before, 407 to 474.35; after, 494 to 559.1): the distances behind transposes fell from 4.58 us for 48 to 3.88 for 40, so 0.09 each, which is near the forecast's 0.109 and not the rival's 0.03. Behind products of 512 columns they fell from 54.78 us for 224 to 54.05 for 216, 0.7 where I had 1.8, since the value and output products stand 0.27 apart where they were 0.23; and behind the 96 score products from 8.0 to 7.2, which I had not foreseen. In this trace a product has no one distance: a query product has 0.27 to another and 0.23 to a score product. Two slips of the prediction changed nothing. With the Trainium skill's formula (56 ns) for the transposes alone that rival is at 2109 and not 2106, which takes over the whole count. And 52 us of GpSimd in a wide batch don't follow from 17.0 and 3.3 in each of four steps, which is 30; 27.8 were measured.

**What of 2095 is left.** With the four causes out, the kernel takes 2115 us, inside my range; but that is another kernel than the one I forecast. Its span lies 47.1 over before's: +85.0 in the context phase, -19.4 in the wide layers (forecast -36.6), -18.5 in the narrow ones. The 17 us of the wide layers are 0.48 us in each of 16 batches (7.7, inside the bound of +9 of a term that I had set to 0) and 9.5 at their borders, 16.1 where I had +6.6.

## What to carry over

Before a new transfer is costed by its bytes, divide its rows: by the rule of experiment 3 the number of DMA engines that it gets is the largest divisor up to 16 of its row count, and the fullest engine can set the time while the mean share looks low. When loads are added to a queue, read what each of its entries waits for in every phase, and who is behind it. And where a step's addition or copy is put off, follow the bank's item order to the next user: an engine with time to spare can still hold the path by one instruction in the wrong place.

## What the runs showed of the hardware

- One DMA engine moved 27 to 28 GB/s with 8 KB rows, and a transfer of 127 rows was on one engine (experiment 3: the mean share was 0.07 in such a slice).
- At the same 259 GB/s the engines were busy for 0.75 of the time with runs of 8 KB and five stores a round (experiment 1), and for 0.88 with runs of 2 KB and 23 stores a round (experiment 2).
- In the kernel after a DMA share of 0.63 went with waits of up to 18.4 us for stores.
- Gaps of 2.1 us in TensorE's work, one in each narrow pair, were followed by half clock in some pairs and not in others (kernel after: granted clock 0.58 from 1106 to 1110 us, 1.00 from 1125.2 to 1138): the even unit took 14.4 or 12.9 us.
